# Sigmoid twice, rounded and into a PSUM bank, and a tail that goes tile by tile, in a recurrent layer's two products

## What is computed

```
h = sigmoid(einsum('bts,st->bs', x, W1) + b1)     # W1 is (1024, 24)
y = h @ W2.T + b2                                 # W2 is (1024, 1024)
```

## Time and profile before

| | |
|---|---|
| median of 3 runs | 313.45 us (312.76 to 313.72) |
| the profiled execution | 314.94 us |
| its span | 313.1 us |
| busy: PE, DVE, ACT, POOL | 83%, 84%, 16%, 64% |
| DMA | 109.48 MB, mean 350 GB/s |
| mean granted clock of TensorE | 0.976 |

### The profile page before, as it was taken

How to read it: one execution, slowest core, us unless ns; L and a number is a source line. 1 busy time by engine, 2 the same in 40 slices (tenths; PEclk the granted TensorE clock), 3 DMA queues, 4 the chain that set the end, 5 groups by cost and what they waited for, 6 DMA issues and landing times.

```text
span 313.1 us, 4779 instructions
## 1 busy us (share of the span) xinstructions
PE 260.9 (83%) x1761; PEld 221.4 (71%) x1761; DVE 263.8 (84%) x382; ACT 50.9 (16%) x85; POOL 201.9 (64%) x111
## 2 busy tenths in 40 slices
PE   0838677738886799999996999996999997799985
PEld 0737677638864578888874788885888895588874
DVE  0619999828998999888999998899997899998966
ACT  4111222303244010100060000004101104000030
POOL 2209677626379898984498976466988816999100
PEclk9968999978999999999999999999999999999999
DMA  7999999999999999999999999999999999999207
GB/s 187 398 386 389 385 387 387 402 387 388 386 386 386 388 386 379 385 384 378 345 359 378 272 384 385 387 380 378 374 373 374 373 363 347 334 342 342 69 3 268
DMA packets 67675, 109.48 MB, mean 350 GB/s; under 512 B 3642, under 2 KB 40514, under 8 KB 67652
## 3 DMA queue, kind: packets, MB, share of 16 engines
q1 hardware_dynamic: 67056, 107.06, 96.8%
q10 hardware_dynamic: 596, 2.11, 1.7%
HBM read 104.97 MB, written 4.19 MB: 349 GB/s over the span
## 4 chain that ended last, share of the span: by engine, by line
PE 53%; DMA 19%; issue 13%; DVE 10%; ACT 4%; SPq 1%; DVEq 0%; ACTq 0%
PE xbank L234 26%; PE pbank L303 22%; DMA ring<-in_r_x 19%; DVE acc L356 7%; PE xbank L334 3%; ACT h L442 2%; DVE h_lo L368 1%; DVE w_lo L363 1%; ACT h_hi L467 1%; PE pbank L293 1%; PE pbank L334 1%; PE pbank L263 1%; DVE acc L354 1%; ACT L442 0%; SPq L197 0%
## 5 line engine op out<-in xcount | busy, mean ns | idle before, releaser
L356 DVE SCALAR_TENSOR_TENSOR acc<-xbank,w,acc 128x512 f32<-128x512 f32 x280 | 197.4, 743 | 30.4 <-PE xbank L234 28.4
L234 PE MATMUL xbank<-ident,ring 128*128 128x128 f32 x1184 | 173.3, 281 | 39.6 <-DMA ring<-in_r_x 27.1
L234 PEld LDWEIGHTS xbank<-ident,ring 128*128 128x128 f32 x1184 | 143.5, 145 | 71.9 <-DVE acc L356 26.6
L496 POOL TENSOR_TENSOR nat<-nat,w1all 128x768 f32<-128x768 f32 (+2 forms) x56 | 108.5, 1939 | 79.5 <-DMA nat<-in_r_x 65.6
L506 POOL TENSOR_TENSOR nat<-nat 128x768 f32<-128x768 f32 (+2 forms) x46 | 90.3, 1962 | 3.6
L303 PE MATMUL pbank<-w_hi,h_hi 128*128 128x512 f32 x112 | 48.3, 432 | 1.5 <-ACT h_hi L467 1.4
L303 PE MATMUL pbank<-w_lo,h_hi 128*128 128x512 f32 x112 | 48.3, 431 | 0.0
L303 PE MATMUL pbank<-w_hi,h_lo 128*128 128x512 f32 x112 | 41.0, 434 | 3.7 <-DVE h_lo L368 3.7
L442 ACT ACTIVATE h<-acc,b1col 128x512 f32<-128x512 f32 (+1 forms) x22 | 12.5, 600 | 96.6 <-DVE acc L356 63.2
L303 PEld LDWEIGHTS pbank<-w_hi,h_hi 128*128 128x128 f32 x112 | 21.3, 191 | 3.0 <-ACT h_hi L467 1.3
L454 ACT COPY y<-pbank 128x512 f32<-128x512 f32 x16 | 9.4, 587 | 81.3 <-PE pbank L303 81.3
(11 more groups left out here) (37 smaller groups left out, 93.1 us busy)
## 6 DMA issues: line engine op xcount, KB each, us to landing
ring<-in_r_x SPq DMA_DIRECT2D x38, 1024.0 KB, 13.0
ring<-in_r_x SPq DMA_DIRECT2D x36, 768.0 KB, 9.2
nat<-in_r_x SPq DMA_DIRECT2D x20, 512.0 KB, 13.0
nat<-in_r_x SPq DMA_DIRECT2D x24, 384.0 KB, 9.4
ring<-in_r_x SPq DMA_DIRECT2D x18, 512.0 KB, 6.7
y<-in_L_rec_W SPq DMA_DIRECT2D x2, 2048.0 KB, 15.5
nat<-in_r_x SPq DMA_DIRECT2D x12, 256.0 KB, 7.6
out_y<-y ACTq DMA_DIRECT2D x4, 512.0 KB, 6.6
```

The lines of the kernel that those rows point to most:

```text
L234: mm = pe.transpose(xbank[u % XBANKS][:, j * P:(j + 1) * P], tile, ident[:, :])
L356: nc.vector.scalar_tensor_tensor(out=total, in0=bank, scalar=weight, in1=total, op0=ALU.mult, op1=ALU.add).then_inc(unit_added, 1)
L496: nc.gpsimd.tensor_tensor(slot, slot, row, ALU.mult).then_inc(nat_weighed, 1)
```

## The change

ScalarE now computes each sigmoid twice: once into h_hi, rounded as it is written, and once into a new PSUM bank `hbank`, from which VectorE subtracts h_hi. As there is only one such bank, the second pass waits until VectorE has made the low part before (`h_lo_ready`, or `tail_lo` in the tail). The low part of chunk v now comes at unit v of the next stage. The SBUF tensor h is gone, and b2 is staged in the last slot of `nat`, for which SP waits. `hbank` takes a bank from the transposes (XBANKS 5); `nat` gets a seventh slot, stage 1 sums seven steps on POOL, and the places of stages 0 and 1 change. In the tail the loops are turned: for each output both chunks, six products in a row; h_hi steps wait for `tail_hi`, the h_lo step for `tail_lo`; the eight outputs use five `xbank`, two `pbank` and the first `xbank` again.

```diff
--- before.py
+++ after.py
@@ -18,8 +18,8 @@
 
 
 STAGES = (
-    (0, 0, 4, 4, (2, 3, 5, 7, 9, 11, 13, 15, 17, 18), "keep"),
-    (0, 4, 4, 6, (0, 2, 3, 5, 6, 8, 9, 11, 12, 14, 15, 17), "last"),
+    (0, 0, 4, 4, (2, 3, 5, 7, 9, 11, 12, 13, 15, 16, 17, 18), "keep"),
+    (0, 4, 4, 7, (0, 1, 3, 4, 5, 7, 8, 9, 11, 12, 13, 15), "last"),
     (4, 0, 3, 6, (0, 2, 3, 5, 6, 8, 9, 11, 12, 14, 15, 17), "keep"),
     (4, 3, 3, 6, (0, 2, 3, 5, 6, 8, 9, 11, 12, 14), "add"),
     (4, 6, 2, 6, (1, 2, 3, 4, 5, 6, 8, 9, 10, 11, 12, 13), "last"),
@@ -36,8 +36,8 @@
     LAST = NS - 1
     CMAX = 4
     RING = 5
-    NATS = 6
-    XBANKS = 6
+    NATS = 7
+    XBANKS = 5
 
     REST = 12
     assert (B, T, S, O) == (2 * BANK, 24, 1024, 1024)
@@ -102,7 +102,6 @@
         w_lo = sb("w_lo", [P, SC, O], F32R)
         y = sb("y", [P, JT, O])
         acc = sb("acc", [P, CMAX, BANK])
-        h = sb("h", [P, CMAX, BANK])
         h_hi = sb("h_hi", [P, CMAX, BANK], F32R)
         h_lo = sb("h_lo", [P, CMAX, BANK], F32R)
         w1all = sb("w1all", [P, NK, S])
@@ -114,6 +113,8 @@
         ident = sb("ident", [P, P])
         xbank = [ctx.enter_context(nc.psum_tensor(f"xbank{n}", [P, BANK], F32)) for n in range(XBANKS)]
         pbank = [ctx.enter_context(nc.psum_tensor(f"pbank{n}", [P, BANK], F32)) for n in range(2)]
+
+        hbank = ctx.enter_context(nc.psum_tensor("hbank", [P, BANK], F32))
 
         x_loaded = [sem(f"x_loaded{n}") for n in range(RING)]
         nat_loaded = [sem(f"nat_loaded{n}") for n in range(NATS)]
@@ -154,6 +155,11 @@
             j, oh = divmod(n, OH)
             return j, slice(oh * BANK, (oh + 1) * BANK)
 
+        def tail_bank(n):
+
+            return (xbank[(UNITS + n) % XBANKS] if n < XBANKS else pbank[n - XBANKS] if n < XBANKS + 2
+                    else xbank[(UNITS + n - XBANKS - 2) % XBANKS])
+
         def steps_of(i):
 
             return 3 * chunks[i] + (fate[i] == "keep")
@@ -193,6 +199,9 @@
                             sp.wait_ge(nat_added, sums_made(m - NATS + 2))
                         elif m >= NATS:
                             sp.wait_ge(unit_turned, sum_turned(parts[m - NATS][0]))
+                        if m == NATS - 1:
+
+                            sp.wait_ge(b2_ready, 1)
                         sj, sc, sn = STAGES[s][0] + HALF * f, STAGES[s][1], STAGES[s][2]
                         sp.dma_start(nat[:, m % NATS, :, :sn * P],
                                      x_v[:, sj:sj + HALF, k, sc * P:(sc + sn) * P]).then_inc(nat_loaded[m % NATS], 16)
@@ -320,21 +329,24 @@
             last_steps = OUTS * steps_of(LAST - 1)
             for k in range(last_steps - REST, last_steps):
                 product_step(LAST - 1, k)
-            for c in range(chunks[LAST]):
-                for n in range(OUTS):
-                    j, cols = out_half(n)
-                    if c == 0 and n < XBANKS:
-                        pe.wait_ge(unit_added, UNITS - XBANKS + n + 1)
-                    if c == 0 and n >= XBANKS:
-                        pe.wait_ge(y_added, added_at[LAST] - OUTS + n + 1)
+            for n in range(OUTS):
+                j, cols = out_half(n)
+                bank = tail_bank(n)
+                if n < XBANKS:
+                    pe.wait_ge(unit_added, UNITS - XBANKS + n + 1)
+                elif n < XBANKS + 2:
+                    pe.wait_ge(y_added, added_at[LAST] - 2 + n - XBANKS + 1)
+                else:
+                    pe.wait_ge(y_added, added_at[LAST] + n - XBANKS - 1)
+                for c in range(chunks[LAST]):
                     if n % OH == 0:
-                        pe.wait_ge(tail_lo, c * JT + j + 1)
-                    bank = xbank[(UNITS + n) % XBANKS] if n < XBANKS else pbank[n - XBANKS]
+                        pe.wait_ge(tail_hi, j * chunks[LAST] + c + 1)
                     for k, (a, w) in enumerate(((h_hi, w_hi), (h_hi, w_lo), (h_lo, w_hi))):
+                        if n % OH == 0 and k == 2:
+                            pe.wait_ge(tail_lo, j * chunks[LAST] + c + 1)
                         mm = pe.matmul(bank[:, :], a[:, c, j * P:(j + 1) * P], w[:, STAGES[LAST][1] + c, cols],
                                        start=c == 0 and k == 0, stop=c == chunks[LAST] - 1 and k == 2)
-                    if c == chunks[LAST] - 1:
-                        mm.then_inc(out_summed, 1)
+                mm.then_inc(out_summed, 1)
 
         @block.vector
         def _(dve):
@@ -364,8 +376,8 @@
                                         ALU.subtract).then_inc(w_lo_ready, 1)
 
             def low_part(i, c):
-                dve.wait_ge(h_hi_ready, first_h[i] + c + 1)
-                nc.vector.tensor_tensor(h_lo[:, c, :], h[:, c, :], h_hi[:, c, :].bitcast(F32),
+                dve.wait_ge(h_ready, first_h[i] + c + 1)
+                nc.vector.tensor_tensor(h_lo[:, c, :], hbank[:, :], h_hi[:, c, :].bitcast(F32),
                                         ALU.subtract).then_inc(h_lo_ready, 1)
 
             def add_out(i, n, bank):
@@ -384,31 +396,28 @@
                     if i == 0 and v - 2 in W2S:
                         split_w2(W2S[v - 2])
 
-                    c, odd = divmod(v - chunks[i], 2)
-                    if i > 0 and 0 <= c < chunks[i - 1] and odd == 0:
-                        low_part(i - 1, c)
+                    if i > 0 and v < chunks[i - 1]:
+                        low_part(i - 1, v)
                     if i > 0 and fate[i - 1] != "keep" and v >= 2:
                         for n in range(outs_due(i, v - 2), outs_due(i, v - 1)):
                             add_out(i - 1, n, pbank[n % 2])
 
-            for c in range(chunks[LAST]):
-                for j in range(JT):
+            for j in range(JT):
+                for c in range(chunks[LAST]):
                     rows = slice(j * P, (j + 1) * P)
-                    dve.wait_ge(h_ready, first_h[LAST] + c * JT + j + 1)
-                    nc.vector.tensor_copy(h_hi[:, c, rows], h[:, c, rows]).then_inc(tail_hi, 1)
-                    dve.wait_ge(tail_hi, c * JT + j + 1)
-                    nc.vector.tensor_tensor(h_lo[:, c, rows], h[:, c, rows], h_hi[:, c, rows].bitcast(F32),
+                    dve.wait_ge(h_ready, first_h[LAST] + j * chunks[LAST] + c + 1)
+                    nc.vector.tensor_tensor(h_lo[:, c, rows], hbank[:, :P], h_hi[:, c, rows].bitcast(F32),
                                             ALU.subtract).then_inc(tail_lo, 1)
             for n in range(outs_due(LAST, len(units[LAST]) - 2), OUTS):
                 add_out(LAST - 1, n, pbank[n % 2])
             for n in range(OUTS):
-                add_out(LAST, n, xbank[(UNITS + n) % XBANKS] if n < XBANKS else pbank[n - XBANKS])
+                add_out(LAST, n, tail_bank(n))
 
         @block.scalar
         def _(act):
             act.dma_start(b1row[:, :], b1.rearrange("(c p) -> c p", p=P)).then_inc(b1_loaded, 16)
             for p in (0, 32):
-                act.dma_start(h[p:p + 1, 0:OH, :], b2.rearrange("(a h n) -> a h n", a=1, n=BANK)).then_inc(b2_loaded, 16)
+                act.dma_start(nat[p:p + 1, NATS - 1, :, :], b2.rearrange("(a h n) -> a h n", a=1, n=BANK)).then_inc(b2_loaded, 16)
 
             def keep_set(q):
                 act.wait_ge(set_turned, q + 1)
@@ -428,7 +437,7 @@
             act.wait_ge(b2_zeroed, 1)
             for p in (0, 32):
                 nc.scalar.copy(b2x[p:p + 1, :].rearrange("a (h n) -> a h n", n=BANK),
-                               h[p:p + 1, 0:OH, :]).then_inc(b2_rounded, 1)
+                               nat[p:p + 1, NATS - 1, :, :]).then_inc(b2_rounded, 1)
             for q in range(EARLY):
                 keep_set(q)
             for m in range(SC):
@@ -438,9 +447,18 @@
             for m in range(SC, OH * SC):
                 high_w2(m)
 
-            def sigmoid(i, c, rows):
-                nc.scalar.activation(h[:, c, rows], acc[:, c, rows], ACT.Sigmoid,
-                                     bias=b1col[:, bass.ds(STAGES[i][1] + c, 1)]).then_inc(h_ready, 1)
+            def sigmoid(i, c, rows, tail):
+
+                bias = b1col[:, bass.ds(STAGES[i][1] + c, 1)]
+                nc.scalar.activation(h_hi[:, c, rows], acc[:, c, rows], ACT.Sigmoid,
+                                     bias=bias).then_inc(h_hi_ready if tail is None else tail_hi, 1)
+
+                if tail:
+                    act.wait_ge(tail_lo, tail)
+                else:
+                    act.wait_ge(h_lo_ready, first_h[i] + c)
+                nc.scalar.activation(hbank[:, :rows.stop - rows.start], acc[:, c, rows], ACT.Sigmoid,
+                                     bias=bias).then_inc(h_ready, 1)
 
             act.wait_ge(set_kept, 1)
             act.wait_ge(b2_ready, 1)
@@ -457,17 +475,16 @@
                         act.wait_ge(y_added, OH * (j + 1))
                         act.dma_start(out_v[:, j, :], y[:, j, :]).then_inc(group_stored, 16)
                 if i > 0:
-                    act.wait_ge(h_lo_ready, first_h[i])
```

(20 more changed lines are left out.)

## The result

| | before | after |
|---|---|---|
| median of 11 runs each, the same chip | 313.08 us (312.23 to 314.52) | 314.44 us (313.69 to 316.4) |
| ratio | | 1.005, 95% interval 1.0025 to 1.0074 |
| profiled execution, its span | 314.94, 313.1 us | 315.84, 313.9 us |
| mean granted clock | 0.976 | 0.951 |

The account below looks back on a forecast made before the run. The x stream was taken to set the pace. TensorE terms summed to -4.5 us, stream bound -4.4, less 0.8 taken back: -3.6, tail zero. From median 313.45 this gave 309.9 us, range 308.6 to 313.5.

Parts of the forecast that it names:

- rival (d): Chopped stage changes halve TensorE's clock for some 7 us, costing 3.5 us: 313.4 us; chance 0.05 together with its clock.
- the stream's floor: End of the x stream: with both holes closed, last landing at 288.55 and tail start at 293.2 us.
- The 0.8 us taken back: Allowance on the sum, because two chains taking turns add waits to each other: -4.4 becomes -3.6 us.
- Loop and pass: One-bank hand-over at stage changes: second sigmoid pass into PSUM 0.72 us, gap per turn 0.80 us.
- Rival (c): Hand-over of the one bank decides: a second pass 0.5 us dearer makes the kernel slower, 315.7 us; chance 0.12.
- Change 0 to 1 (-1.4): Stage change 0 to 1: TensorE reaches unit 17 at 108.8 instead of 110.2 us, a gain of 1.4.
- stage 1 (-2.0): Seven steps summed on POOL: four units fewer, products spread over 49 units instead of 52, saving 2.0 us.
- Stage 0 (+1.4): Two more x transfers in stage 0, one ahead of an x item TensorE awaits, costing 1.4 us.
- Change 1 to 2 (-0.7): Stage change 1 to 2: TensorE reaches unit 14 at 172.4 instead of 173.10 us, a gain of 0.7.
- Change 2 to 3 (+1.2): Stage change 2 to 3: TensorE has unit 9 at 220.5 instead of 219.3 us, a loss of 1.2.
- Change 3 to 4 (-3.0): Stage change 3 to 4: first product needing h_lo at 268.2 instead of 271.17 us, a gain of 3.0.
- Tail: After the last stage: first y store 8.2 us after the tail's start, products done before stores need them; net zero.

Follow-up runs that it names:

- a_same: The changed kernel again, unaltered, timed beside the kernel before: 314.7 us, ratio 1.0043.
- a_warm: Changed kernel plus idle TensorE products after units 4 to 7 of stage 1 and 4 and 5 of stages 2 and 3: 312.26 us, ratio 0.9972.
- b_same: The kernel before again, unaltered, for a second profile: 313.62 us, ratio 1.0007.
- b_warm: The kernel before plus the same idle TensorE products in stages 1, 2 and 3, as control: 312.88 us, ratio 0.9987.
- b_bank5: The kernel before with five transpose banks instead of six, the sixth serving only the tail: 312.74 us, ratio 0.9984.
- c_twoacc: Changed kernel with old stage table, acc twice by stage parity, h_hi passes first, low part c at unit 2 + 2c: 312.14 us, ratio 0.9973.
- a_warm1: Changed kernel plus idle TensorE products only after units 4 to 7 of stage 1: 312.42 us, ratio 0.9987.
- a_oldtable: Changed kernel with the old stage table (six POOL steps in stage 1, old places, six nat slots): 314.15 us, ratio 1.003.
- c_warm: Changed kernel with old table, two accs and VectorE's tail additions reordered, plus idle TensorE products late in stage 2 and early in stage 3: 311.43 us, ratio 0.9928.

## Why the prediction was wrong

**The step that failed first is rival (d), the clock.** It was dismissed because "in this trace the stage changes ran at 1.00 throughout". That was the old order, where the windows of before are these:

```profile
96.00:98.00 2.00, 1.55 (x11) 1.13 (x11) 1.48 (x3) 1.27 (x3) 2.00 (x2) 1.00 1.03 384
98.00:100.00 2.00, 1.59 (x10) 1.01 (x8) 2.00 (x2) 0.00 (x0) 2.00 (x1) 1.00 1.05 385
100.00:102.00 2.00, 0.49 (x5) 0.49 (x5) 2.00 (x3) 0.00 (x0) 1.92 (x2) 1.00 1.05 383
```

One of them is thin, 0.49 us of work, and the clock stayed at 1.00; in the changed kernel three thin ones follow one another (0.66, 0.76, 0.73). a_same has one of 0.34, from 214 to 216 us, at 1.00 too, so a single thin window does not tell. The prediction's own terms had the new one: a unit of 0.44 us per loop turn of 1.26 + 0.80 = 2.06 us for units 6 to 8. The measured turn is 2.18, with 0.66 to 0.76 us of work in each two. From a_same to a_warm (314.7 to 312.26) it cost 2.4 us, 2.0 of it in stage 1; the rival said 3.5. The Trainium skill ("TensorE: Matmul & The Clock Gate", section "HAM oscillation — how this bites in real kernels") tells of a kernel in which TensorE waits for a load after each block of products, for longer than the block took, and is re-throttled before every next block. The trace agrees at the change 0 to 1, where TensorE waits 1.33, 1.52 and 1.27 us for VectorE around single units of 0.44 us: the fall is in each of the four profiles of the changed order without idle products. At the later changes it is not every time (a_same has one fall, after three).

**The second is the base of the sum.** The stall to be removed was read from the one profiled execution and subtracted in full from the median, which stood 1.5 us below it. With the 3.6 us taken off, the profiled execution starts its tail at 294.0; an execution at the median would have to start it at about 292.5, earlier than the 293.2 that the prediction itself gives as the stream's bound. Three other profiles of before or its near copies (b_same, b_warm, b_bank5) start the tail at 296.77, 295.61 and 294.09, not 297.61, and have cheaper low parts. In these four, the faster an execution is, the less of lag it has to lose. The prediction took the mean of 1592 ns, and the 1.00 of one change, as the low part's cost, where it depends on POOL's operation beside it.

**The third is the stream's floor.** It was set at a last landing of 288.55 and a tail start of 293.2. With all holes closed (c_twoacc) the last x can be used at 289.32 and the tail starts at 294.04. The 0.8 us taken back for another reason happen to cover this, which is luck. Against the tail start of b_warm, 295.61 in an execution near the median, at most 1.6 us were to be had, not 4.4. c_twoacc, a_warm, a_warm1 and b_bank5 all end within 0.1 to 0.8 us of the median of before beside them.

Of the 4.5 us between the forecast of 309.9 and the 314.44 measured, the clock took some 2.4 and the base 1.5. The rest is what a_warm's profiled execution, 311.97, stands above the 311.3 forecast for such an execution.

Point by point:
- Loop and pass: right (0.83 and 0.67 to 0.69 against 0.80 and 0.72). Rival (c) did not occur. The Trainium skill ("ScalarE: Activation LUTs", section "Step-by-step: what each stage is for") says that ScalarE writes PSUM with less latency than SBUF: the pass at 0.67 to 0.69 beside 0.71 to 0.72, and 0.37 beside 0.39 in the tail, agree, by 0.02 to 0.05.
- Change 0 to 1 (-1.4) and stage 1 (-2.0): their sum is right at full clock. a_warm's stage 1 takes 63.01 against 63.0. That it meets so closely is luck: unit 17 came 17.5 us after the first sigmoid, 16.7 forecast, the table alone measured -1.55, and the 66.40 of before holds a low part of 2.72 us (b_warm's stage 1, with one of 0.68, takes 64.12). At the granted clock only 1.2 of the 3.4 stayed.
- Stage 0 (+1.4): the size is right (+1.5 between a_oldtable and a_same).
- Change 1 to 2 (-0.7): wrong, +0.1 in a_warm and +0.8 in after. Change 2 to 3 (+1.2): +0.5 without a fall, +1.75 with one.
- Change 3 to 4 (-3.0): the step itself was right. The first h_lo product runs 7.81 us after the sigmoid (270.01, 262.20) against 10.85 before and 7.9 forecast. But the stage's length fell by 0.7 and 0.2 only, since TensorE then waits for the last x. The gain went into that wait.
- The lost bank, the POOL parts and b2: nothing, as said. POOL's last sum of stage 1 starts at 135.85 and nobody waits for it.
- Tail: 7.92 us to the first store, 8.2 forecast, 8.28 before. The end comes 15.1 us after the tail's start, 15.5 before. That the products end 11.8 us after the start was right, that the stores need them later was not: the last addition waited 0.35 us for them.

Both bounds of the sum were drawn at 293.1 and 293.2, and the stage lengths of a_warm add up near the first one until stage 3 (its first sigmoid of stage 4 at 257.83, 258.8 forecast). What the loop saved on VectorE was real, and the chip took it back as clock, as waits for x, and as a gain that the faster executions of before already had.

## What to carry to other kernels

Write down how busy TensorE will be in each few microseconds of the new schedule, not only how long the stall lasts: a row at full clock vouches only for a stretch of work as dense as its own. Take the stall to be removed from several executions, and make the sum against the floor of the resource that is never idle. A saving on another engine ends there. Where a subtraction reads two SBUF inputs beside POOL's operations, look at when it meets them and not at its mean. And ask of each clock fall whether TensorE is behind or ahead of that resource; in these runs only the first kind was worth idle products.

## What the runs showed that was not expected

- The same instruction, with the same operands, took 0.68 to 2.73 us in before and its near copies: the first low part of stage 0 takes 2.72 in before, 2.73 in b_same, 1.40 in b_bank5 and 0.68 in b_warm. Nearly every one ended 0.55 us after the operation of POOL that it met. Read from PSUM all fourteen average 682 ns.
- Executions of before differ by up to 3.6 us within one group. Of the 13 beside c_warm, nine took 312.74 to 313.45 us and four 314.64 to 315.18, with mean clocks of 0.956 to 0.982 and 0.978, so the clock does not separate them. The 35 beside a_same lie from 311.37 to 314.99 without such a gap.
- b_warm's stage 1 is shorter than before's (64.12 against 66.40 us) though both run it at clock 1.00. Its first low part of 0.68 instead of 2.72 us would account for 2.0 of the 2.3 (b_same, with 2.73, takes 66.13, and b_bank5, with 1.40, 65.26). It began 0.11 us before POOL's operation ended. Such a meeting can shift with the idle products or from one execution to the next, and so b_warm is a weaker control than it looks: in the changed kernel, whose low parts don't vary, this doubt does not arise.
